# The hidden rows between the up and the down stage of a mixture-of-experts layer: turned by DMAs and a VectorE block transpose in place of TensorE

## What is computed

```python
def _swiglu(t, wa, wb, wo):
    h = jax.nn.silu(t @ wa.T) * (t @ wb.T)
    return h @ wo.T
t = x.reshape(-1, DIM)                                  # 2048 x 512, normalized
scores = jax.nn.softmax(t @ gate_w.T, axis=-1)          # 16 experts
weights, indices = jax.lax.top_k(scores, TOP_K)         # 2 of them
for e in range(N_EXPERTS):
    w_e = jnp.sum(jnp.where(indices == e, weights, 0.0), axis=-1)
    y = y + _swiglu(t, w1[e], w3[e], w2[e]) * w_e[:, None]
z = _swiglu(t, sw1, sw3, sw2)                           # two shared experts of 352
return (y + z).reshape(shape)
```

## Time and profile before

| | us |
|---|---|
| median of 3 runs (741.28 to 747.87) | 741.99 |
| span of the profiled execution, first to last instruction | 739.8 |
| PE busy in it | 717.1 |
| DVE busy | 568.5 |
| ACT busy | 459.4 |
| POOL busy | 363.4 |

### The profile page before, as it was taken

How to read it: one execution, slowest core, us unless ns; L and a number is a source line. 1 busy time by engine, 2 the same in 40 slices (tenths; PEclk the granted TensorE clock), 3 DMA queues, 4 the chain that set the end, 5 groups by cost and what they waited for, 6 DMA issues and landing times.

```text
span 739.8 us, 15553 instructions
## 1 busy us (share of the span) xinstructions
PE 717.1 (97%) x4602; PEld 676.3 (91%) x4602; DVE 568.5 (77%) x1111; ACT 459.4 (62%) x659; POOL 363.4 (49%) x190
## 2 busy tenths in 40 slices
PE   3999999999999999999999999999999999999998
PEld 3999999999998999899989999988989999999997
DVE  7899999999965578428899588848987699679942
ACT  6575757575432222126878588847885789578931
POOL 4999888887401065042435433543634354434320
PEclk9999999999999999999999999999999999999999
DMA  6678687877522122463667577766565764432101
GB/s 231 215 239 288 218 272 216 279 218 253 186 85 60 29 43 29 144 197 90 161 201 218 131 232 210 198 176 168 145 182 160 176 193 90 74 68 46 30 1 57
DMA packets 48404, 114.88 MB, mean 155 GB/s; under 512 B 7472, under 2 KB 8624, under 8 KB 48336
## 3 DMA queue, kind: packets, MB, share of 16 engines
q1 hardware_dynamic: 35792, 89.67, 37.1%
q0 software_dynamic: 12544, 24.40, 17.9%
HBM read 157.78 MB, written 29.26 MB: 253 GB/s over the span
## 4 chain that ended last, share of the span: by engine, by line
PE 69%; DVE 13%; DMA 6%; issue 5%; ACT 3%; SPq 1%; ACTq 1%; POOL 1%; DVEq 1%; POOLq 0%
PE pair L1303 19%; PE bank L1303 15%; PE pair L1328 12%; PE pair L1234 8%; PE bank L1328 6%; PE bank L1185 4%; PE pair L1311 3%; DMA out<-ys,slot_info 3%; DMA raw<-in_weights 2%; PE bank L1245 2%; DVE prod L829 2%; DVE bank L834 2%; DVE x L800 2%; DVE w_lo L1150 1%; DVE rows L841 1%
## 5 line engine op out<-in xcount | busy, mean ns | idle before, releaser
L1150 DVE TENSOR_TENSOR w_lo<-raw,w_hi 128x1408 fp32r<-128x1408 f32 x94 | 148.5, 1621 | 47.0 <-ACT w_hi L733 47.0
L1441 POOL DMA_INDIRECT out<-ys,slot_info x47 | 80.6, 1714 | 120.6 <-ACT ys L721 87.3
L1428 POOL DMA_INDIRECT tn<-t_rows,slot_info x47 | 75.5, 1605 | 123.1 <-DVE tT_lo L888 90.6
L733 ACT ACTIVATE w_hi<-raw 128x1408 fp32r x94 | 124.6, 1374 | 2.1 <-issue 1.4
L1234 PE MATMUL pair<-kv_hi,toep_hi 128*128 128x288 f32 x320 | 100.6, 314 | 1.7 <-DMA toep_lo<-kpad_lo 1.4
L1234 PE MATMUL pair<-kv_lo,toep_hi 128*128 128x288 f32 x320 | 95.3, 298 | 0.0
L1234 PE MATMUL pair<-kv_hi,toep_lo 128*128 128x288 f32 x320 | 95.1, 297 | 0.0
L1155 DVE TENSOR_TENSOR w_lo<-raw,w_hi 128x1536 fp32r<-128x1536 f32 x47 | 82.3, 1752 | 4.5 <-ACT w_hi L740 4.5
L1379 POOL TENSOR_TENSOR kv_lo<-kv,kv_hi 128x2304 fp32r<-128x2304 f32 x15 | 77.3, 5153 | 5.9 <-ACT kv_hi L625 5.9
L740 ACT ACTIVATE w_hi<-raw 128x1536 fp32r x47 | 69.3, 1474 | 0.1
L829 DVE TENSOR_TENSOR prod<-pair,q 128x256 f32<-128x256 f32 x128 | 53.4, 417 | 15.1 <-PE pair L1234 9.6
(11 more groups left out here) (223 smaller groups left out, 2009.3 us busy)
## 6 DMA issues: line engine op xcount, KB each, us to landing
raw<-in_weights SPq DMA_DIRECT2D x94, 704.0 KB
raw<-in_weights SPq DMA_DIRECT2D x47, 768.0 KB
toep_hi<-kpad_hi SPq DMA_DIRECT2D x15, 512.0 KB, 4.6
toep_lo<-kpad_lo SPq DMA_DIRECT2D x15, 512.0 KB, 6.2
cx<-in_ctx SPq DMA_DIRECT2D x15, 384.0 KB, 6.3
stage<-in_weights SPq DMA_DIRECT2D x16, 272.0 KB, 6.7
xt<-in_x SPq DMA_DIRECT2D x16, 256.0 KB, 6.4
xr<-in_x SPq DMA_DIRECT2D x16, 256.0 KB, 6.6
```

The lines of the kernel that those rows point to most:

```text
L733: act.activation(w_hi[s % 2][:, a:b], raw[:, bass.ds(half + a, b - a)], ACT.Copy).then_inc(hi_ok[n_], 1)
L1150: dve.tensor_tensor(w_lo[s % 2][:, a:b], raw[:, bass.ds(half + a, b - a)], w_hi[s % 2][:, a:b].bitcast(F32), ALU.subtract).then_inc(lo_ok[ ...
L1428: pool.indirect_dma_start(out=tn[o % 3][:], out_offset=None, in_=t_rows, in_offset=bass.IndirectOffsetOnAxis(ap=slot_info[:, 3 * i:3 * i + ...
L1441: pool.indirect_dma_start(out=out, out_offset=bass.IndirectOffsetOnAxis(ap=rows, axis=0), in_=ys[o % 2][:], in_offset=None, bounds_check=R ...
```

## The change

The three PE transposes per unit, their PSUM bank and `turn_hidden` go. In their place:

- ACT issues four DMAs (`spread_hidden`) that copy hid into a new buffer `spread`: DMA g takes the 88 hidden columns g*88 to g*88+87 of all 128 rows and lays them on the 32 partitions 32g to 32g+31, four rows side by side, so each piece is 88 numbers (352 bytes), 128 pieces per DMA. It stands in step n behind the two w_hi pieces, and waits for hid of unit n-1 and for `hid_turned` of unit n-2 (spread has one buffer).
- DVE transposes spread in blocks of 32 x 32 back into hid, 384 columns (`dve.transpose`), and signals `hid_turned`. It stands behind the product hid of unit n in DVE's step n, and waits for the four DMAs (`hid_spread`).
- hT_hi (ACT) now copies from hid in SBUF, and waits for that signal.
- hT_lo stays on DVE for the 20 units ahead of the first routed one and goes to POOL, behind the adding scatter, for the other 59.
- silu of unit n waits for hT_lo of unit n-2 (hid is now in use until then). The rows of the down weights are laid out on the host in the matching order, with 8 zero rows per 88.

```diff
+            def spread_hidden(m):
+                act.wait_ge(hid_ok, m + 1)
+                wait(act, hid_turned, m)
+                for g in range(4):
+                    act.dma_start(spread[32 * g:32 * g + 32, :].rearrange("p (t c) -> p t c", t=4)[:, :, 0:QUAD],
+                                  hid[m % 2][:, g * QUAD:(g + 1) * QUAD]).then_inc(hid_spread, 16)
...
+                if unit(n - 1):
+                    spread_hidden(n - 1)
                 if (s := split_down_at(n)) is not None:
...
                 if unit(n):
-                    wait(act, hid_turned, n - 1)
-                    if n < 2:
-                        act.wait_ge(hid_zero, 2)
+                    wait(act, hTl_ok, n - 1)
                     act.wait_ge(up_ok, n + 1)
                     act.activation(hid[n % 2][:, 0:INTER], h_bank(n)[0][:, 0:INTER], ACT.Silu).then_inc(silu_ok, 1)
                 if unit(n - 1):
                     m = n - 1
                     wait(act, down_ok, m - 1)
                     act.wait_ge(hid_turned, m + 1)
-                    act.activation(hT_hi[m % 2][:], ps_ht[:, 0:IPAD], ACT.Copy).then_inc(hTh_ok, 1)
+                    act.activation(hT_hi[m % 2][:], hid[m % 2][:], ACT.Copy).then_inc(hTh_ok, 1)
...
                 if unit(n - 1):
                     m = n - 1
-                    dve.wait_ge(hTh_ok, m + 1)
-                    dve.tensor_tensor(hT_lo[m % 2][:], ps_ht[:, 0:IPAD], hT_hi[m % 2][:].bitcast(F32),
-                                      ALU.subtract).then_inc(hTl_ok, 1)
+                    dve.wait_ge(hid_spread, 64 * (m + 1))
+                    dve.transpose(view(hid[m % 2][:], 0, [[1, 4], [P, ICH], [4, 32]]),
+                                  view(spread[:], 0, [[QPAD, 4], [32, ICH], [1, 32]])).then_inc(hid_turned, 1)
+                    if m < FIRST_R:
+                        dve.wait_ge(hTh_ok, m + 1)
+                        dve.tensor_tensor(hT_lo[m % 2][:], hid[m % 2][:], hT_hi[m % 2][:].bitcast(F32),
+                                          ALU.subtract).then_inc(hTl_ok, 1)
...
-            def turn_hidden(n):
-                wait(pe, hTl_ok, n)
-                pe.wait_ge(hid_ok, n + 1)
-                for c in range(ICH):
-                    last = pe.transpose(ps_ht[:, c * P:(c + 1) * P], hid[n % 2][:, c * P:(c + 1) * P], ident[:])
-                last.then_inc(hid_turned, 1)
...
                 if (o := done_at(n)) is not None:
                     add_out(o)
+                if unit(n - 1) and n - 1 >= FIRST_R:
+                    m = n - 1
+                    wait(pool, hTl_ok, m)
+                    pool.wait_ge(hTh_ok, m + 1)
+                    pool.tensor_tensor(hT_lo[m % 2][:], hid[m % 2][:], hT_hi[m % 2][:].bitcast(F32),
+                                       ALU.subtract).then_inc(hTl_ok, 1)
```

More of the change, by code:

```diff
@@ L46 @@
 IPAD = ICH * P
+QUAD, QPAD = INTER // 4, IPAD // 4
 W2 = ICH * L
@@ L179, in program @@
         ps_o, ps_q, ps_t, ps_rows = bank[4], bank[5], bank[6], bank[7]
-        ps_h, ps_ht, ps_y = [[bank[0], bank[1]], [bank[4], bank[5]]], bank[2], [bank[3], bank[7]]
+        ps_h, ps_y = [[bank[0], bank[1]], [bank[4], bank[5]]], [bank[3], bank[7]]
         ps_gate = ps_t[:, 0:EXPERTS]
@@ L229, in program @@
         hid = sb2("hid", [P, IPAD])
+        spread = sb("spread", [P, IPAD])
         hT_hi = sb2("hT_hi", [P, IPAD], F32R)
@@ L295, in program @@
         up_ok, silu_ok, hid_ok = sem("up_ok"), sem("silu_ok"), sem("hid_ok")
-        hid_turned, hTh_ok, hTl_ok, down_ok = sem("hid_turned"), sem("hTh_ok"), sem("hTl_ok"), sem("down_ok")
+        hid_spread, hid_turned, hTh_ok, hTl_ok, down_ok = sem("hid_spread"), sem("hid_turned"), sem("hTh_ok"), sem("hTl_ok"), sem("down_ok")
         y_ok = sem("y_ok")
@@ L896, in _ @@
             dve.wait_ge(conv_ok, 8 * TILES)
-            dve.memset(hid[0][:, INTER:IPAD], 0.0).then_inc(hid_zero, 1)
-            dve.memset(hid[1][:, INTER:IPAD], 0.0).then_inc(hid_zero, 1)
-            dve.wait_ge(hid_zero, 2)
+            dve.memset(view(spread[:], QUAD, [[QPAD, 4], [1, QPAD - QUAD]]), 0.0).then_inc(hid_zero, 1)
+            dve.wait_ge(hid_zero, 1)
             count = [0]
@@ L1334, in _ @@
                     up(unit(n))
-                if unit(n - 1):
-                    turn_hidden(n - 1)
                 for o in prepares_at(n):
@@ L1478, in down @@
     def down(w2):
-        w = np.zeros((w2.shape[0], IPAD, L), w2.dtype)
-        w[:, :INTER] = w2.transpose(0, 2, 1)
-        return w.reshape(-1, ICH, P, L).transpose(0, 2, 1, 3).reshape(-1, P, W2)
+        w = np.zeros((w2.shape[0], 4, QPAD, L), w2.dtype)
+        w[:, :, :QUAD] = w2.transpose(0, 2, 1).reshape(-1, 4, QUAD, L)
+        return w.reshape(-1, 4, ICH, 32, L).transpose(0, 1, 3, 2, 4).reshape(-1, P, W2)
     sw1, sw3 = (a("L0_ffn_" + n).reshape(SHARED, INTER, L) for n in ("sw1", "sw3"))
```

## The result

The changed kernel takes 875.69 us (median of 4 runs, 872.12 to 879.04), the kernel before 741.63 on the same chip: 1.179 times as long, 95% interval 1.173 to 1.185. The forecast was 839 us in a range of 795 to 940: slower, as said, and 37 us more than said. The profiled span went from 739.8 to 872.0 us.

The account below looks back on a forecast made before the run. PE bounded the kernel before; the change would close a ring of waits between ACT and DVE, 9.0 us per routed step. Terms +91, -8, -4, +3, +15 sum to +97 on 739.8: span 837, time 839 us, range 795 to 940.

Parts of the forecast that it names:

- The ring: Routed steps: ACT's hT_hi waits for DVE's transpose, DVE for ACT's next weight pieces; 9.0 us per step, chance 0.78.
- The signs named ahead: Changed profile: PE about 85%, ACT idle some 2.5 us before hT_hi, DVE likewise before first w_lo, transpose hardly waiting.
- The transpose: DVE's new 384-column transpose, not in the trace: taken as 0.55 us, bounds 0.45 to 1.1.
- taken as hidden in routed steps: ACT's four DMA issues, 1.95 us, run beside weight pieces; if not hidden, 1.35 us per routed step, 62 in all.
- The middle stretch: 342 to 705 us: 46 routed steps of 9.0 and 8 shared of 5 make 454 us against 363, +91.
- the fill: Behind the first shared units, weights split ahead let about three routed steps go at PE's pace: -8 us.
- The late landings: Middle stretch: one routed step in three sees a DMA landing 1 us over the 4.5: +15 us.
- Units ahead: Shared units ahead of the routed ones: PE's saving at best 20 times 0.33 = -6.6 us; taken as -4.
- the second ring: Through DMA issue and landing L: 4.5 + L in routed steps, hidden; the only ring in shared steps, 5.6 to 6.0 us.
- POOL's hT_lo at nothing: hT_lo on POOL, 1.04 us, hidden under PE's up; by the skill's port rule collisions could add up to 48 us.
- Rival 4: PE's clock falls to its lower level as PE idles in routed steps; up to 1,060 us, chance 0.03.
- Rival 3: DMA landings set the pace: at L = 6.3 routed steps take 10.8 us, 955 us, chance 0.13.

Follow-up runs that it names:

- experiment 1: Kernel before, with only one added wait: hT_hi also waits for DVE's hid of the same step, no DMA or DVE transpose; 790.64 us against 742.13.
- experiment 2: Changed kernel with the four DMAs per unit left out, so the transpose turns zeros; 831.42 us, ratio 1.119.
- experiment 4: Changed kernel with hT_lo of all units back on DVE, none on POOL; 876.31 us.
- experiment 8: Changed kernel with hT_hi one step later, ys at the end of ACT's step, and the four DMAs left out; 767.13 us, ratio 1.036.
- experiment 7: Changed kernel with DVE's transpose moved ahead of the third weight piece and of hid, from the first routed unit on; 856.89 us, ratio 1.155.
- experiment 5: Changed kernel with ACT's hT_hi one step later, behind the next step's weight pieces and DMA issues; 900.01 us, ratio 1.215.
- experiment 6: Changed kernel with hT_hi one step later and ys moved to the end of ACT's step; 844.82 us, ratio 1.138.

## Why the prediction was right, and where its terms were off

*The ring, the term that decided: right.* Predicted 9.0 us per routed step, measured 9.25 in the step shown and 9.12 as the median of the long ones. The signs named ahead are there: PE at 85%, hT_hi idle for 2.86 us with the transpose as its releaser, hardly a wait of the transpose itself. One came at half its size: DVE idles 1.26 us before its first w_lo, not some 2.5, as another 1.14 us of its idle time stands before tT_lo. That the order alone closes the ring is shown by experiment 1, where it turns in 8.33 us without any added work; the 0.8 us up to 9.12 are about the transpose's link (0.96 in place of a hand-over of 0.1). The terms missed by 35 us of span in all, nearly all on one side: 19 ahead of the routed units, 15 in the middle stretch, 1 at the end. The range held because it had room for issues that are not hidden.

*The transpose: mis-sized.* "I take 0.55" for an operation not in the trace; it takes 0.87 us, within the bounds given (0.45 to 1.1). With the hand-over the link is 0.96 instead of 0.65, +0.31 per step; the shorter links around it leave +0.23 of that on the ring.

*DMA issues "taken as hidden in routed steps": half right.* Four take 2.5 us, not 1.95. They part the third weight piece from the first two in 42 of 47 steps, a sign that the prediction had named against its sum, but ACT idles there for 24.9 us in all, not the 62 that the other bound gave. The chain of waits in the changed kernel passes through them in steps such as this one (start, us, what):

```profile
574.41 0.62 ACTq L730
...
576.41 1.49 ACT w_hi L752
...
578.16 1.75 DVE w_lo L1164
...
580.35 0.80 DVE hid L1173
```

That way round, through the issues and the third piece, is about as long as the way through DVE's first two low parts, so removing the issues alone leaves the other way: experiment 2 still shows a step of 9.13.

*The middle stretch: +98 forecast for 54 steps, +113 measured over 55.* The 47 long steps average 9.14 us, late landings included, 7 us in all over the forecast of 9.0. The eight short ones average 6.5 us instead of 5, +12. And the fill, "about three routed steps go at PE's pace", did not come, +8: the first three steps took 9.1, 9.4 and 9.0 us. The late landings, put at +15 as a term of their own, are in the 24 us that the DMAs cost there; that term made up for part of the others, which was luck.

*Units ahead: "I take -4", measured +15.* This is the largest miss. Leaving the DMAs out brings 12 of the 19 us back, so the second ring, through issue and landing, was longer than the 5.6 to 6.0 us that were taken: issues 2.5 instead of 1.95, the transpose 0.87, and in the stretch from 220 to 342 us seven transposes that waited 11.3 us for their DMA, one of them 6.4. The step that failed is "it is the only ring" for a shared step: DVE also works out the routing there, and that work now stands in front of a transpose for which ACT waits. The starts of silu jump there by 8.3 us, from 3.1 behind the kernel before at the 11th unit to 11.4 at the 12th. In the changed kernel (timelines of POOL, DVE and ACT):

```profile
275.23 2.75 POOL L1464 TENSOR_TENSOR field<-field,prow 128x1536 bf16<-128x1536 bf16 x1
...
275.62 2.77 DVE L1177 TENSOR_TENSOR hT_lo<-hid,hT_hi 128x384 fp32r<-128x384 f32 x1 [0.65 <-ACT hT_hi L762]
...
281.48 7.47 DVE L1033 TENSOR_TENSOR place<-iob,slotb 128x1024 bf16<-128x1024 bf16 x2
...
290.23 0.52 ACT L762 ACTIVATE hT_hi<-hid 128x384 fp32r<-128x384 f32 x1 [11.35 <-DVE hid L1173]
```

and at the same place in the kernel before (DVE):

```profile
270.07 0.55 DVE L1164 TENSOR_TENSOR hT_lo<-pair,hT_hi 128x384 fp32r<-128x384 f32 x1
...
273.02 7.47 DVE L1024 TENSOR_TENSOR place<-iob,slotb 128x1024 bf16<-128x1024 bf16 x2
```

The routing table `place` takes DVE 7.47 us in both. Before, hT_hi waited for PE alone and started at 275.71 us, beside it; now hT_hi waits 11.35 us for the transpose behind it, the longest of the 79 waits. It is the same wait that closes the ring in the routed steps. Without the DMAs the jump is still there, 6.2 us from the 11th to the 13th unit. A smaller part has to do with where hT_lo reads: with two SBUF inputs beside POOL's operation it took 2.77 us, with a PSUM input, beside the same operation, 0.55. That happened to one of the 20 hT_lo; the others took 0.56. The Trainium skill ("SBUF — State Buffer", section "Who interferes with whom") says that a VectorE instruction with two SBUF inputs contends with a GpSimd instruction that reads SBUF; the trace agrees, as hT_lo ended 0.4 us after POOL's operation.

*POOL's hT_lo at nothing: right.* 1.00 us measured, 1.04 forecast, and no gain from taking it back (experiment 4). The 48 us of collisions that the prediction set against it did not come in the changed kernel: all 59 of POOL's hT_lo took 0.99 to 1.02 us, since DVE waits when POOL works there. In the kernels in which DVE no longer waits, they do collide: in experiment 8 the row on POOL takes 2.12 us, and DVE's two up pieces 3.94 instead of 3.16.

*The end: +3 forecast, +3.7 measured. Rival 4, PE's clock:* the granted clock is 0.95 in the middle stretch and fell 18 times in the span, once before; but PE has only 13 of the 460 us of the chain of waits between 370 and 830 us, so it costs this kernel next to nothing. *Rival 3, landings,* was wrong as the limit of this kernel, but it is the limit right behind, as experiment 7 shows.

## What to carry to other kernels

Before moving work from a full engine to others, write down for each in-order engine what a new wait would hold up behind it, and follow that chain until it either ends or comes back: a wait for a result that another engine delivers last in its step, placed ahead of what that engine needs first, closes a ring whose length is the sum of the links on the way round, here 9.25 us, more than any engine's own work in a step. A step that was to fall from 6.66 to 6.33 us on its busiest engine became 9.1 to 9.3 us, with every engine idle part of the time. And when a limit is removed, look in the same trace for the next one: here the ring, ACT's row and the landings lay within 1 or 2 us of each other, so single cures won little, and one (experiment 5) built a new ring.

## What was not expected of the hardware

- A DMA issue on ACT took 0.55 to 0.67 us in most cases (median 0.62, up to 1.1 in the changed kernel), against 0.47 on SP in the earlier trace rows (0.35 as the median of all of SP's issues there). In experiment 6 ACT's arithmetic stood idle for 1.9 of the 2.5 us that four of them took.
- A block transpose of 128x384 f32 on DVE takes 0.87 us, where a subtraction of the same shape takes 0.55 to 0.56.
- POOL's and DVE's instructions with two SBUF inputs stretch each other: POOL's hT_lo 1.00 us alone, 2.07 to 2.12 beside w_lo; DVE's hT_lo 0.56 alone, 2.77 beside POOL's field.
